# A GNN kernel in which the message layers of nine "early" half units and the histogram of the hot groups are put in another order on four engines

## The reference, cut to what matters

```python
h = x
hs, hd = h[src], h[dst]
e = concatenate([hs, hd], axis=1)
a_k = exp(relu(e @ W_att_k + b_att_k))            # k = 1, 2, 3
att_k = segment_sum(a_k, dst, N)
avg_a = (a1/att1[dst] + a2/att2[dst] + a3/att3[dst]) / 3
m = avg_a * relu(relu(relu(hs @ W1 + b1) @ W2 + b2) @ W3 + b3)
h_neigh = segment_sum(m, dst, N) / maximum(deg, 1)
out = relu(concatenate([h, h_neigh], 1) @ W_c1 + b_c1) @ W_c2 + b_c2
return layernorm(x + out)
```

## Time and profile before

| | |
|---|---|
| median of 3 runs | 831.94 us (829.34 to 834.98) |
| the profiled execution | 827.13 us |
| its span | 823.1 us |
| PE busy | 685.3 us (83%) |
| DVE busy | 589.1 us (72%) |
| ACT busy | 419.8 us (51%) |
| POOL busy | 571.6 us (69%) |

### The profile page before, as it was taken

One profiled execution on the slowest core, in us unless ns is written; L12 is line 12 of the kernel. 1 busy time (PEld: TensorE's weight loads), 2 busy tenths in 40 slices (PEclk: granted clock), 3 DMA queues, 4 the chain that ended last, 5 costly groups with the idle time before them and its releaser, 6 DMA issues.

```text
span 823.1 us, 17406 instructions
## 1 busy us (share of the span) xinstructions
PE 685.3 (83%) x5133; PEld 534.5 (65%) x5133; DVE 589.1 (72%) x1943; ACT 419.8 (51%) x1048; POOL 571.6 (69%) x605
## 2 busy tenths in 40 slices
PE   9933899999698777899998988888788888779875
PEld 5732566666366444698787777777676667657664
DVE  5883667676677678677777777677667777787766
ACT  6556566666555342677777767664123322332323
POOL 7777776555544677777777777777777777777760
PEclk9975777778777677699999999999889999898898
DMA  7873333222652223333333333333434343343321
GB/s 234 244 186 74 80 80 77 63 63 63 58 43 54 55 66 94 73 87 76 87 77 84 79 80 77 82 80 91 108 91 115 101 106 102 103 132 99 100 57 33
DMA packets 82741, 75.14 MB, mean 91 GB/s; under 512 B 34872, under 2 KB 66400, under 8 KB 82640
## 3 DMA queue, kind: packets, MB, share of 16 engines
q0 software_dynamic: 19008, 39.82, 22.1%
q1 hardware_dynamic: 63344, 34.00, 14.9%
q10 hardware_dynamic: 288, 0.13, 0.1%
HBM read 64.62 MB, written 9.26 MB: 90 GB/s over the span
## 4 chain that ended last, share of the span: by engine, by line
PE 27%; DVE 23%; POOL 18%; issue 16%; ACT 7%; DMA 6%; DVEq 2%; SPq 1%; ACTq 0%
POOL work L1224 18%; PE bank L1405 7%; DVE fin L1730 7%; ACT bank L1518 4%; DMA hot_logit<-early_rows 3%; DVE counts L1708 2%; PE bank L1426 2%; DVE acc L1851 2%; PE bank L881 2%; DVE fin L1695 2%; PE bank L1409 2%; DMA work<-message_table,src_t 2%; PE bank L1361 2%; PE bank L599 2%; PE bank L1379 1%
## 5 line engine op out<-in xcount | busy, mean ns | idle before, releaser
L1224 POOL DMA_INDIRECT work<-message_table,src_t x558 | 530.8, 951 | 214.5 <-issue 164.6
L1405 PE MATMUL bank<-work 128*128 128x144 f32 (+8 forms) x1188 | 235.9, 329 | 38.5 <-DVE acc L1851 38.3
L1405 PEld LDWEIGHTS bank<-work 128*128 128x128 f32 x1188 | 186.1, 222 | 60.0 <-issue 45.8
L1579 ACT COPY work<-bank 128x192 f32<-128x192 f32 (+7 forms) x126 | 37.3, 296 | 189.2 <-DVE work L1803 189.0
L1443 PE MATMUL bank<-work,fin 128*128 128x129 f32 (+1 forms) x882 | 114.7, 286 | 0.0
L1851 DVE TENSOR_TENSOR acc<-acc,bank 128x192 f32 (+8 forms) x297 | 88.7, 299 | 30.4 <-issue 7.5
L1518 ACT ACTIVATE bank<-hot_logit 128x384 f32<-128x384 f32 (+1 forms) x147 | 72.7, 494 | 69.2 <-DVE fin L1730 60.2
L1443 PEld LDWEIGHTS bank<-work,fin 128*128 128x128 f32 (+1 forms) x882 | 105.5, 197 | 2.1
L1834 DVE TENSOR_TENSOR work<-bank,work 128x576 f32<-128x576 f32 (+7 forms) x126 | 86.2, 684 | 13.5 <-DVE work L1829 0.5
L1730 DVE SCALAR_TENSOR_TENSOR fin<-bank,counts 128x384 f32<-128x384 f32 (+1 forms) x147 | 81.4, 554 | 17.3 <-ACT bank L1518 16.4
L1409 PE MATMUL bank<-work 128*4 128x48 f32 (+8 forms) x1188 | 92.9, 203 | 0.0
(11 more groups left out here) (150 smaller groups left out, 811.1 us busy)
## 6 DMA issues: line engine op xcount, KB each, us to landing
work<-message_table,src_t POOLq DMA_INDIRECT x558
side<-near_nodes SPq DMA_DIRECT2D x102, 48.0 KB
side<-logit_parts SPq DMA_DIRECT2D x297, 0.8 KB
message_table<-work SPq DMA_DIRECT2D x12, 262.0 KB, 3.8
work<-message_table SPq DMA_DIRECT2D x48, 65.5 KB
work<-in_x_t SPq DMA_DIRECT2D x12, 256.0 KB, 4.0
fin<-in_x SPq DMA_DIRECT2D x11, 256.0 KB, 3.1
logits_or_x<-in_x_t SPq DMA_DIRECT2D x11, 256.0 KB
```

The lines of the kernel that those rows point to most:

```text
L1224: pool.indirect_dma_start(out=rows_of(n)[:, t, :], out_offset=None, in_=table[:, :], in_offset=bass.IndirectOffsetOnAxis(ap=src_t[:, h, g: ...
L1405: pe.matmul(sums[:, at:at + HEADS * w], rows_here[:, t, 0:P], wt_of(i)[:, t, :], start=h == 0, stop=h == TILES - 1)
```

## The change

Early units become 3, 5, ... 19 (before 4, 6, ... 20). On PE the order of a step with early work becomes:

- even step i = 2k: `add_edges(i)`, `count_edges(i)`, `turn_early(k)`, `edge_q(i + 2)`, `first_early(k)`
- odd step i = 2k + 1: `add_edges(i)`, `second_early(k)`, `count_edges(i)`, `edge_q(i + 2)`, `third_early(k)`

On ACT `hidden_early(k, 0)` moves ahead of `low_hots` in odd steps. On SP `load_early` moves from behind the near and q loads of its step to ahead of them. On DVE the four `add_counts` of the step before and the four groups of `one_hots` alternate, one group of each in turn.

```diff
-EARLY_FROM, EARLY_EVERY = 4, 2
+EARLY_FROM, EARLY_EVERY = 3, 2
...
                     for at in range(-AHEAD, n_steps):
+                        if first and at > 0 and at % EARLY_EVERY == 0 and at // EARLY_EVERY < EARLY:
+                            load_early(at // EARLY_EVERY)
                         while loaded < n_units and taken(loaded, NEAR) <= at + 1:
                             load_near(loaded)
                             loaded += 1
                         if at + AHEAD + Q_RING - 2 < n_units:
                             load_q(at + AHEAD + Q_RING - 2)
-                        if first and at > 0 and at % EARLY_EVERY == 0 and at // EARLY_EVERY < EARLY:
-                            load_early(at // EARLY_EVERY)
...
-                        if i + 2 < n_units and not (first and i < COUNT_STEPS):
-                            edge_q(i + 2)
-                        if k is not None and i % EARLY_EVERY == 0 and k >= 1:
-                            third_early(k - 1)
                         if k is not None and i % EARLY_EVERY == 1 and k < EARLY:
-                            first_early(k)
+                            second_early(k)
                         if first and i < COUNT_STEPS:
                             count_edges(i)
                         if k is not None and i % EARLY_EVERY == 0 and k < EARLY:
                             turn_early(k)
+                        if i + 2 < n_units:
+                            edge_q(i + 2)
+                        if k is not None and i % EARLY_EVERY == 0 and k < EARLY:
+                            first_early(k)
                         if k is not None and i % EARLY_EVERY == 1 and k < EARLY:
-                            second_early(k)
-                        if i + 2 < n_units and first and i < COUNT_STEPS:
-                            edge_q(i + 2)
+                            third_early(k)
...
+                        k = early_turn(i)
+                        if k is not None and i % EARLY_EVERY == 1 and k < EARLY:
+                            hidden_early(k, 0)
                         if first and i < COUNT_STEPS:
                             low_hots(i)
-                        k = early_turn(i)
...
                         if k is not None and i % EARLY_EVERY == 1 and k < EARLY:
-                            hidden_early(k, 0)
                             hidden_early(k, 1)
...
+                    def count_step(i):
+
+                        for j in range(PAIRS):
+                            if 0 <= (i - 1) * PAIRS + j < n_hot:
+                                add_counts((i - 1) * PAIRS + j)
+                            if i * PAIRS + j < n_hot:
+                                one_hots(i * PAIRS + j)
...
-                        if first and 0 <= i - 1 < COUNT_STEPS:
-                            add_counts(i - 1)
-                        if first and i < COUNT_STEPS:
-                            one_hots(i)
+                        if first and i <= COUNT_STEPS:
+                            count_step(i)
```

More of the change, by code:

```diff
@@ L1685, in _ @@
                     hot_window = window_registers(dve, n_hot, lambda g: hot_nodes - width_of(g))
[L1687 to L1696, removed]
@@ L1698, in add_counts, with one_hots @@
-                    def add_counts(step):
-                        if step == 0:
-                            dve.wait_ge(s_zero, zeroed)
[L1701 to L1709, removed]
+                    def one_hots(g):
+                        n = width_of(g) * n_blocks
+                        if g >= PAIRS:
+                            dve.wait_ge(s_ct, (g - PAIRS + 1) * TILES)
+                        for h in range(TILES):
+                            t = g * TILES + h
+                            dve.tensor_scalar(hot_comb[:, t % HOT_RING, 0:n], iota16[:, 0:n],
+                                              comb_t[:, g, h:h + 1], None, ALU.is_equal).then_inc(s_oh, 1)
@@ new lines, in add_counts @@
+                    def add_counts(g):
+                        if g == 0:
+                            dve.wait_ge(s_zero, zeroed)
+                        w = width_of(g)
+                        start = hot_window(g)
+                        dve.wait_ge(s_ct, (g + 1) * TILES)
+                        if g >= 1:
+                            dve.wait_ge(s_cadd, g)
+                        here = counts[:, :, bass.ds(start, w)]
+                        dve.tensor_tensor(here, here, bank[COUNT_BANKS[g % FOUR]][:, 0:w * n_blocks].rearrange(
+                            "p (b d) -> p b d", d=w), ALU.add).then_inc(s_cadd, 1)
```

## The result

| | before | changed |
|---|---|---|
| median | 830.64 us (829.33 to 834.98, 4 runs) | 799.08 us (794.54 to 821.68, 4 runs) |
| ratio of the compared runs | | 0.9593, 95% interval 0.9512 to 0.9674 |
| the profiled execution, its span | 827.13, 823.1 us | 795.49, 791.6 us |
| PE's granted clock, mean | 0.856 | 0.885 |

The change takes 31.6 us off by the medians and 31.5 us off the span; the forecast was 24. The ratio leaves out one slow run of the changed kernel, 821.68 us at a granted clock of 0.843 against 0.875 to 0.888 in the other three, and gives 4.1%, about 34 us. The granted clock is the mean share of its full 2.4 GHz at which TensorE (PE) ran.

The account below looks back on a forecast made before the run. POOL's gather train, released by `add_edges(22)` at 311.92 us, sets the end; savings in steps 0 to 22 count fully. Terms 9.6, 8, 2.5, 4 and 0 us make 24 us: 831.9 - 24 = 808 us, range 792 to 828 us.

Parts of the forecast that it names:

- The end follows POOL's waits one for one: POOL's waits for PE: time off steps 0 to 22 comes off the end one for one, up to 47 us.
- The sum: The gains over steps 0 to 22 added up: 24 us off 831.9 us, giving 808 us.
- six pairs (2, 3) to (12, 13): Loop of PE and DVE: 18.4 us a pair with the clock falling once each, 9.6 us gained.
- DVE's floor: DVE's own work in a pair of steps: at least 17.6 us, about 16.5 for three pairs with narrow groups.
- The first rival: PE's clock stays at 2.4 GHz in the pairs: 35 us gained, 797 us; chance 0.17.
- my own case: The whole kernel: PE's clock still falls once a pair, 808 us, case range 800 to 815 us; chance 0.35.
- slower rival: Three small PE stops in a pair keep the clock low longer: 14 us more, 846 us; chance 0.07.
- The alternation: On DVE, one-hots between two `add_counts` remove the 0.20 us self-wait: 0.6 us off each step.
- The third rival: On DVE, alternating gives nothing and the 0.20 us gaps stay: 16 us gained, 816 us; chance 0.10.
- The reload: PE's 12.3 us of weight-load waits for the reload: all hidden but block 7, up to 2 us left there.
- the second: PE's turn waits for `rows_early` where it waited for the reload: 11 us gained, 821 us; chance 0.18.
- The fifth: PE's clock low for 17 us of a pair around the even step's seam: 846 us; chance 0.07.

Follow-up runs that it names:

- Run 10: The changed kernel with DVE's additions ahead of its one-hots again, under the first comparison's conditions: 819.04 us, ratio 0.9889 to the kernel before.
- run 8: The kernel before with five idle filler matmuls on PE in the stop before each turn, on the slower chips: ratio 0.9958.
- run 2: The changed kernel with DVE's additions ahead of its one-hots again, on the slower chips: ratio 0.9919 to the kernel before.
- runs 1 and 11: The kernel before with only DVE's alternation of count additions and one-hots added, twice, on the slower chips: ratios 1.0016 and 1.0005.
- run 9: The changed kernel as it is, on chips where the kernel before takes 1,010 to 1,012 us: ratio 0.9779 to the kernel before.

## Why the prediction was right

The measured 799.1 us lies in the range of 792 to 828 us, the sign was right, and the gain was larger than forecast. By its own steps:

**The end follows POOL's waits one for one.** Right: waits down by 30.4 us, span by 31.5 us. The run without the alternation is near the same line (waits for PE 49.6 to 46.2 us, span 823.1 to 818.5 us). Not right is that the end hangs on `add_edges(22)`: the last release is that of `add_edges(20)` at 261.87 us, where I had named 288 us, and `add_edges(22)` ends at about 280.3 us, 1.6 us before the gather that needs it. Some of what steps 21 and 22 gained no longer counts.

**The sum.** Against the rows of both kernels:

| term | forecast | measured |
|---|---|---|
| six pairs (2, 3) to (12, 13) | 9.6 us | 120.0 - 102.1 = 17.9 us |
| pair (14, 15) | 8 us | 27.45 - 18.40 = 9.1 us |
| pair (16, 17) | 2.5 us | 22.05 - 20.47 = 1.6 us |
| steps 18 to 22 | 4 us | 49.7 - 46.5 = 3.2 us |
| steps 0 and 1 | 0 us | step 2 starts at 94.09 instead of 92.53 us: -1.6 us |

The terms come to 24 us forecast and 30.2 measured. The one that was mis-sized is the first: 17.0 us a pair in place of 18.4. The step behind it was "I expect the clock still to fall once a pair, since the stretch of three-column matmuls stays". It fell in three of the six pairs. The second step that failed is DVE's floor, 17.6 us a pair and about 16.5 with narrow groups: pairs (2, 3) and (4, 5) took 15.3 and 15.6 us with DVE busy 12.45 and 12.83 us of them, and the wide pair (8, 9) 17.15 us. The floor was read as the length of two steps of DVE's timeline and so held its stops. (The odd step's parts, 6.4 and 1.8 us, also sum to 8.2 and not to 8.4.) Steps 0 and 1 lie outside the bounds of 1 us that I gave them: PE now runs layer one of block 0, 2.07 us at the low clock, ahead of step 1.

The first rival, that the clock stays up, had a chance of 0.17 and named 797 us in all and 16.2 us for the first term. Measured are 799.1 and 17.9 us, and a mean clock of 0.92 in the pairs, where "above 0.9" was its sign. So the result is nearer to this rival than to my own case, and that the range held the measured time is in part the width of the range.

**What lets the clock fall.** Not the three-column matmuls by themselves. The changed kernel passes them at the end of steps 3, 7, 11, 15 and 17 without a fall. PE's timeline at the end of step 7, behind which the clock stays at 2.4 GHz:

```profile
138.82 0.68 PE L1426 MATMUL bank<-fin 128*128 128x294 bf16 x4 [0.18 <-ACT fin L1556]
139.43 0.29 PE L1357 MATMUL bank<-side 48*128 48x33 bf16 x5
```

and at the end of step 9, behind which it falls:

```profile
154.70 1.12 PE L1426 MATMUL bank<-fin 128*128 128x441 bf16 x4 [0.41 <-ACT fin L1556]
156.59 0.27 PE L1357 MATMUL bank<-side 48*128 48x33 bf16 x5 [0.77 <-DVE work L1840]
...
160.41 1.13 PE L1405 MATMUL bank<-work 128*128 128x72 f32 x4
```

The four 72-column matmuls that cost 1.13 us here cost 0.67 us behind step 11. The falls at 125, 159 and 194 us (the last inside `edge_q` itself) all follow a wait of `edge_q` for `weights` (0.28 us with 0.36 us for ACT before it, 0.77 us with 0.41 us, 0.77 us); the five odd steps whose `edge_q` did not wait for DVE (3, 7, 11, 15, 17) were passed without a fall. Run 10 divides its odd steps in the same way. Its falls behind steps 5, 11 and 13 follow

```profile
126.09 1.66 PE L1426 MATMUL bank<-fin 128*128 128x294 bf16 x8 [0.43 <-DVE fin L1694]
128.43 0.27 PE L1357 MATMUL bank<-side 48*128 48x29 bf16 x5 [0.69 <-DVE work L1833]
...
194.32 0.27 PE L1357 MATMUL bank<-side 48*128 48x33 bf16 x5 [0.79 <-DVE work L1833]
...
215.04 0.27 PE L1357 MATMUL bank<-side 48*128 48x33 bf16 x5 [0.56 <-DVE work L1833]
```

and steps 3 and 15, with 0.18 us and nothing, were passed. The kernel before had 0.81 + 0.49 = 1.3 us of stops ahead of the early `edge_q` of step 12, and 1.0 to 1.8 us in all six pairs. My reading that a stop for the reload belongs to every fall was wrong: in steps 8 and 10 the turn did not wait for the reload, and the clock fell all the same. Step 8:

```profile
157.18 0.92 PE L1426 MATMUL bank<-fin 128*128 128x441 bf16 x4 [1.00 <-ACT fin L1558]
158.01 0.66 PE L1372 MATMUL bank<-ident,hot_logit 128*128 128x128 f32 x4
```

That the falls go with the stops is shown by these rows and by run 8; that the stops alone decide is not. The Trainium skill's page "TensorE: Matmul & The Clock Gate", section "A second HAM failure mode: psum-queue depth-cycling", says that frequent short stops between groups of matmuls make the clock swing; these rows agree, with stops of 0.64 to 1.2 us together before the falls of the changed kernel and 0 to 0.36 us with none. I had used it for the slower rival alone; it bore as much on the gain, since the change makes the stops fewer and shorter.

**The alternation.** Wrong in size, in two ways. By itself it shortens DVE's block by 1.0 us a step (5.15 to 4.2), not 0.6: the self-waits go, and at each change from one kind to the other the next instruction starts about 0.08 us before the last one's end. And it was costed as DVE time, 8 us at the most; without it the new order gives 1.1% instead of 4.1%. Under the other conditions, where all three were measured, the new order alone gives 0.8% (run 2), the alternation alone nothing (runs 1 and 11), both together 2.2% (run 9). So it is shown that the parts don't add and that the clock is higher with both. How the one leads to the other is not. That DVE's `weights` come 1 us earlier and so shorten PE's stop before `edge_q` would fit, but where `edge_q` waited in run 10 it waited for 0.56 to 0.79 us, and in the changed kernel for 0.28 to 0.77: the stops are rarer with the alternation (3 of 8 odd steps, 3 of the 5 that run 10 reached at the high clock) rather than much shorter. The third rival said that the gaps stay. It is refuted: with an instruction of another kind between two additions the 0.20 us is gone (21.8 to 8.3 us of idle time before L1706), so the gap belongs to an addition that waits for the one before it and not to every instruction. The Trainium skill's page "VectorE: DVE Perf Modes", section "The DRAIN you can't avoid", says that a semaphore after each operation costs nothing extra; this case differs where each operation waits for the one before, with 0.20 us between two.

**The reload.** Right on the whole: of eight waits of PE's weight loads with 12.3 us, one of 3.3 us is left, at block 8, which keeps the matmuls 2.83 us. The forecast had left a rest to block 7, which had none. The last hot stores are now issued from 209.07 to 212.2 us and block 8's reload at 214.80 us; in the kernel before 11 us lay between them, and block 8 waited 1.69 us. The hidden reload is a small part of the gain in the six pairs: PE's matmuls had waited for it there 2.45 us in all (0.47, 0.82, 0.67 and 0.49 us in four of the six).

**The second and fifth rival.** The turn waits for nothing in eight of nine pairs, so the second did not occur. The fifth names something real, seen in the run without the alternation: two pairs nearly all at the low clock, of 23.8 and 23.7 us, where it had 22.7 us for 17 us of low clock and 26 us of PE's work at the low clock alone.

**Open.** Why the clock stayed low for two whole pairs in run 10, with PE never idle in them for more than 0.35 us, while after its falls in the changed kernel's pairs it came back within about 10 us; why steps 18 to 22 run at a mean clock of 0.71 in both kernels; and what makes PE pause on the chips where the kernel takes 1,010 us.

## What to carry to other kernels

When two engines hand work to each other in a loop, look at what stops PE for half a microsecond just before a stretch of small matmuls: the stop itself is cheap, the lower clock behind it cost 2 us a pair of steps here where it came back at once and 6.5 us where it did not. Two changes on different engines that give 1% and nothing by themselves can be worth more together; test them apart and together before dropping one. And find first which engine's waits carry the end: here one number, POOL's true waits, gave the span's change to 1 us.

## What the runs showed of the hardware

- In a chain of DVE additions on one tile 0.20 us lie between two of them, put down to the wait for the one before; with an independent instruction between, the wait is gone, and a 441-column one-hot starts 0.09 us before the addition in front ends (151.65 against 151.12 + 0.62).
- Pair (8, 9) took 17.15 us at 2.4 GHz with PE busy 15.55 us, and 23.66 us in run 10, nearly all of it at 1.2 GHz (mean 0.57), with PE busy 23.32 us: halving the clock made PE's work 1.5 times as long and not twice.
- The same kernel took 830 us on some chips and 1,010 us on others, with POOL's gathers as long as before (951 ns) and PE pausing in its stream.
